# Expert rows in tiles of 256 and of 128 rows, and the second tile's weights loaded ahead of the wait for rows

## The reference

```
logits = x @ Wr.T                                  # 8 experts
scores = softmax(logits); the best two of 8 are kept
g = silu(x @ Wg[e].T); u = x @ Wu[e].T             # 512 -> 352 each
out_e = (g * u) @ Wd[e].T                          # 352 -> 512
routed = sum over the two kept experts of score * out_e
shared = (silu(x @ Wsg.T) * (x @ Wsu.T)) @ Wsd.T   # 704 hidden channels
x + gb * (routed + shared)
```

## Time and profile before

| | us |
|---|---|
| median of three runs | 1813.94 |
| the three runs | 1813.15, 1813.94, 1815.92 |
| span of the profiled execution | 1812.5 |
| PE busy | 1708.2 (94%) |
| DVE busy | 1336.2 (74%) |
| ACT busy | 768.1 (42%) |

### The profile page before, as it was taken

How to read it: one execution, slowest core, us unless ns; L and a number is a source line. 1 busy time by engine, 2 the same in 40 slices (tenths; PEclk the granted TensorE clock), 3 DMA queues, 4 the chain that set the end, 5 groups by cost and what they waited for, 6 DMA issues and landing times.

```text
span 1812.5 us, 28335 instructions
## 1 busy us (share of the span) xinstructions
PE 1708.2 (94%) x9093; PEld 1481.3 (82%) x9093; DVE 1336.2 (74%) x2564; ACT 768.1 (42%) x1151; POOL 413.5 (23%) x503
## 2 busy tenths in 40 slices
PE   5499999999779999999999998999999999999998
PEld 0388888888568888888887887999999999998888
DVE  4899999997588777787777654666666666666772
ACT  2333333333245454544454313555545555443331
POOL 0244444442122111322322340000000000004740
PEclk9699999999889999999999999999999999999999
DMA  8432222221624433645554696777767777665861
GB/s 333 132 130 87 78 90 93 87 75 64 212 99 151 154 126 122 215 170 185 182 193 172 226 350 239 269 247 269 258 244 263 247 269 258 243 242 170 293 214 38
DMA packets 141638, 339.31 MB, mean 187 GB/s; under 512 B 20664, under 2 KB 20664, under 8 KB 136048
## 3 DMA queue, kind: packets, MB, share of 16 engines
q1 hardware_dynamic: 110864, 250.68, 40.4%
q10 hardware_dynamic: 20448, 54.01, 7.9%
q0 software_dynamic: 10240, 33.56, 5.3%
HBM read 230.40 MB, written 107.79 MB: 187 GB/s over the span
## 4 chain that ended last, share of the span: by engine, by line
PE 78%; DVE 9%; DMA 6%; issue 3%; ACT 2%; SPq 1%; POOL 1%; ACTq 0%; DVEq 0%; POOLq 0%
PE bank L595 20%; PE bank L597 19%; PE bank L596 19%; PE bank L606 6%; PE bank L2106 4%; PE bank L2104 4%; PE bank L2105 3%; PE bank L2099 2%; DMA out<-raw 1%; DVE k_lo L1591 1%; DVE hid L1677 1%; DMA stage<-in_w_k 1%; ACT sg_t L1238 1%; DMA base<-xres_rows 1%; PE bank L2088 1%
## 5 line engine op out<-in xcount | busy, mean ns | idle before, releaser
L595 PE MATMUL bank<-gu_hi,ex_x_hl 128*128 128x352 f32 x1136 | 378.6, 333 | 1.9 <-DVE gu_lo L1873 1.8
L597 PE MATMUL bank<-gu_hi,ex_x_hl 128*128 128x352 f32 x1136 | 366.9, 323 | 0.0
L596 PE MATMUL bank<-gu_lo,ex_x_hl 128*128 128x352 f32 x1136 | 366.8, 323 | 0.0
L1677 DVE TENSOR_TENSOR hid<-bank,sg_t 128x352 f32<-128x352 f32 x142 | 74.4, 524 | 224.3 <-ACT sg_t L1238 224.3
L595 PEld LDWEIGHTS bank<-gu_hi,ex_x_hl 128*128 128x128 f32 x1136 | 214.4, 189 | 2.4 <-DVE gu_lo L1873 2.1
L596 PEld LDWEIGHTS bank<-gu_lo,ex_x_hl 128*128 128x128 f32 x1136 | 214.5, 189 | 0.0
L597 PEld LDWEIGHTS bank<-gu_hi,ex_x_hl 128*128 128x128 f32 x1136 | 214.0, 188 | 0.0
L1115 POOL DMA_INDIRECT raw<-expert_out_rows,out_slots x64 | 75.2, 1175 | 590.8 <-DMA expert_out_rows<-y_rows 567.8
L1238 ACT ACTIVATE sg_t<-bank 128x352 f32<-128x352 f32 x142 | 66.0, 465 | 273.1 <-PE bank L597 272.8
L2104 PE MATMUL bank<-dn_hi,hid_hi 128*128 128x512 f32 x426 | 170.4, 400 | 9.1 <-DVE hid_lo L1681 9.1
L2106 PE MATMUL bank<-dn_hi,hid_lo 128*128 128x512 f32 x426 | 168.7, 396 | 0.0
(11 more groups left out here) (230 smaller groups left out, 3879.6 us busy)
## 6 DMA issues: line engine op xcount, KB each, us to landing
raw<-in_ex_gu SPq DMA_DIRECT2D x39, 1408.0 KB, 6.9
raw<-in_ex_dn SPq DMA_DIRECT2D x39, 512.0 KB, 7.6
ex_x<-expert_in_rows SPq DMA_DIRECT2D x78, 256.0 KB, 2.8
expert_out_rows<-y_rows ACTq DMA_DIRECT2D x78, 256.0 KB, 4.0
h_rows<-h_t SPq DMA_DIRECT2D x64, 256.0 KB, 2.3
h_turned<-h_hl ACTq DMA_DIRECT2D x32, 512.0 KB
ex_x_hl<-h_turned ACTq DMA_DIRECT2D x32, 512.0 KB, 3.3
x_t<-in_x SPq DMA_DIRECT2D x32, 256.0 KB, 2.6
```

The lines of the kernel that those rows point to most:

```text
L595: pe.matmul(acc, act_hi[i], w_hi[i], start=(i == 0), stop=False)
L596: pe.matmul(acc, act_hi[i], w_lo[i], start=False, stop=False)
L597: last = pe.matmul(acc, act_lo[i], w_hi[i], start=False, stop=(i == chunks - 1))
L1677: dve.tensor_tensor(hid[:, half, 0:F], PS_U[bank][:, 0:F], sg_t[:], ALU.mult).then_inc(u_vec.sem_of["hid"], 1)
```

## The change

There are still 31 tiles of 256 rows (pairs), and 9 tiles of 128 rows (singles) join them: 71 units and 40 tiles instead of 78 and 39. Tiles 0 to 29 are pairs, 30 to 38 singles, 39 a pair. Each expert's rows are padded to a multiple of 128, its even part fills pairs as long as there are any, the rest goes to singles; the tables are computed for both kinds. The padding zeros are 128 rows per expert. Each tile's two parts of weights have semaphores of their own. Tile 1's weights are loaded in front of the wait for rows. The loop becomes a written-out list of units, in which `split_places` says in which unit each piece of weights is split, and on which side of `hid`. The buffers that the gathered outputs use are swapped (`cb_y1`, `cb_y2` to `raw[0]`, `cb_out` to `raw[1]`).

```diff
-NJ = (2 * N + E * (R - 1)) // R
-NU = NJ * R // P
+NU = (2 * N + E * (P - 1)) // P
+NPAIR = 2 * N // R - 1
+NSINGLE = NU - 2 * NPAIR
+NJ = NPAIR + NSINGLE
...
+def is_single(j):
+    return NPAIR - 1 <= j < NJ - 1
...
+LAST_OF = {j: units_of(j)[-1] for j in range(-2, NJ + 2)}
+FIRST_OF = {j: units_of(j)[0] for j in range(NJ + 2)}
+def split_places():
+    hi_first, hi_middle, lo_before, lo_after = ({u: [] for u in UNIT} for _ in range(4))
+    hi_first[ROUTED0 - 1].append((0, "gu"))
+    lo_before[ROUTED0 - 1].append((0, "gu"))
+    for j in range(NJ + 2):
+        u = FIRST_OF[j]
+        alone = is_single(j) or j >= NJ
+        if j and (is_single(j - 1) or j - 1 >= NJ):
+            hi_first[u].append((j, "dn"))
+            lo_after[u].append((j, "dn"))
+            if j + 1 < NJ + 2:
+                hi_middle[u].append((j + 1, "gu"))
+                lo_before[u + 1].append((j + 1, "gu"))
+        elif alone:
+            hi_first[u].append((j + 1, "gu"))
+            lo_before[u].append((j + 1, "gu"))
+        else:
+            hi_first[u].append((j + 1, "gu"))
+            lo_after[u].append((j + 1, "gu"))
+        if not alone:
+            hi_first[u + 1].append((j + 1, "dn"))
+            lo_after[u + 1].append((j + 1, "dn"))
+    return hi_first, hi_middle, lo_before, lo_after
...
@@ SP
             sp.wait_ge(route_done, 1)
-            load_expert(FIRST)
+            load_gu(0)
+            load_dn(0)
             sp.wait_ge(pads_zero, 1)
             for e in range(E):
                 pad_rows(e)
+            load_gu(1)
+            load_dn(1)
...
+            def routed_step(unit):
+                if unit.k + 3 < NU:
+                    load_rows(unit.k + 3)
+                if unit.begins and unit.load < FU:
+                    load_base(unit.load)
+                elif unit.begins and SPLIT <= unit.load < NT:
+                    load_residual(unit.load)
+                for j, part in LO_BEFORE[unit.u] + LO_AFTER[unit.u]:
+                    if j + 2 < NJ + 2:
+                        (load_gu if part == "gu" else load_dn)(j + 2)
...
@@ ACT
+            for u in range(ROUTED0, LATE0):
+                unit = UNIT[u]
+                for piece in HI_FIRST[u]:
+                    expert_hi(*piece)
+                if unit.k + 1 < NU:
+                    routed_x_hi(unit.k + 1)
+                hidhi(u - 1)
+                for piece in HI_MIDDLE[u]:
+                    expert_hi(*piece)
+                silu(u, unit.slot)
...
@@ DVE, tables
+            def running(values, out):
+                link(dve.tensor_tensor(summed[:], upto[:], values[:].to_broadcast([P, E, E]), ALU.mult))
+                link(dve.tensor_reduce(out[:, 0, :], summed[:], AX.X, ALU.add))
...
             def tile_tables():
-                cur = count["end" if E.bit_length() % 2 else "end2"]
+                padded, paired, single = (count[name] for name in ("padded", "paired", "single"))
+                pair_end, single_end = count["pair_end"], count["single_end"]
+                link(dve.tensor_tensor(single[:], padded[:], paired[:], ALU.subtract))
+                running(single, single_end)
+                link(dve.tensor_scalar(step_single[:], padded[:], -1.0, float(REGION), ALU.mult, ALU.add))
+                link(dve.tensor_tensor(step_single[:, :, 0:E - 1], step_single[:, :, 0:E - 1], paired[:, :, 1:E], ALU.add))
+                link(dve.tensor_scalar(step_single[:, :, E - 1:E], step_single[:, :, E - 1:E], float(SPARE_PAIRS * R), None,
+                                       ALU.add))
                 dve.wait_ge(table_const, 1)
-                link(dve.tensor_tensor(below[:], cur[:].to_broadcast([P, NJ, E]), first_row[:], ALU.is_le))
+                for ends, steps_of, p0, p1 in ((pair_end, step_pair, 0, NPAIR), (single_end, step_single, NPAIR, NJ)):
+                    here = [P, p1 - p0, E]
+                    link(dve.tensor_tensor(below[:, p0:p1, :], ends[:].to_broadcast(here), first_row[:, p0:p1, :], ALU.is_le))
+                    link(dve.tensor_tensor(steps_below[:, p0:p1, :], below[:, p0:p1, :], steps_of[:].to_broadcast(here),
+                                           ALU.mult))
                 link(dve.tensor_reduce(eid_f[:, :, 0], below[:], AX.X, ALU.add))
                 link(dve.tensor_scalar(eid_f[:], eid_f[:], float(E - 1), None, ALU.min))
                 link(dve.tensor_copy(eid[:], eid_f[:, :, 0]))
-                link(dve.tensor_tensor(steps_below[:], below[:], step[:].to_broadcast([P, NJ, E]), ALU.mult))
                 link(dve.tensor_reduce(row_f[:, :, 0], steps_below[:], AX.X, ALU.add))
                 link(dve.tensor_tensor(row_f[:, :, 0], row_f[:, :, 0], first_row[:, :, 0], ALU.add))
+                link(dve.tensor_tensor(row_f[:, NPAIR:NJ, :], row_f[:, NPAIR:NJ, :],
+                                       paired[:, :, 0:1].to_broadcast([P, NSINGLE, 1]), ALU.add))
+                begin_pair, begin_single = shift["pair"], shift["single"]
+                link(dve.tensor_tensor(begin_pair[:], pair_end[:], paired[:], ALU.subtract))
+                link(dve.tensor_tensor(begin_single[:], single_end[:], single[:], ALU.subtract))
+                link(dve.tensor_tensor(single_from[:], region[:], paired[:], ALU.add))
+                link(dve.tensor_scalar(begin_single[:], begin_single[:], float(NPAIR * R), None, ALU.add))
+                link(dve.tensor_tensor(begin_single[:], begin_single[:], pair_end[:], ALU.subtract))
+                link(dve.tensor_tensor(begin_pair[:, :, 1:E], single_end[:, :, 0:E - 1], padded[:, :, 0:E - 1], ALU.subtract))
+                link(dve.tensor_scalar(begin_pair[:, :, 1:E], begin_pair[:, :, 1:E], -1.0, -float(NPAIR * R + REGION),
+                                       ALU.mult, ALU.add))
+                link(dve.tensor_tensor(begin_pair[:, :, 1:E], begin_pair[:, :, 1:E], pair_end[:, :, 0:E - 1], ALU.add))
                 dve.tensor_copy(row_of_tile[:], row_f[:, :, 0]).then_inc(route_done, 1)
             def result_slots():
                 past = y_rows[:, 1, :].rearrange("p (n e) -> p n e", e=E)
+                every = [P, 2 * NT, E]
                 link(dve.tensor_copy(slot_f[:, :, 0], flat(slots[:])))
-                link(dve.tensor_scalar(next_region[:], region[:], float(REGION), None, ALU.add))
-                link(dve.tensor_tensor(past, slot_f[:].to_broadcast([P, 2 * NT, E]),
-                                       next_region[:].to_broadcast([P, 2 * NT, E]), ALU.is_ge))
-                link(dve.tensor_tensor(past, past, step[:].to_broadcast([P, 2 * NT, E]), ALU.mult))
-                link(dve.tensor_reduce(flat(route["sc"][:]), past, AX.X, ALU.add))
-                link(dve.tensor_tensor(slot_f[:, :, 0], slot_f[:, :, 0], flat(route["sc"][:]), ALU.subtract))
+                for froms, name, added in ((region, "pair", "sc"), (single_from, "single", "ex")):
+                    link(dve.tensor_tensor(past, slot_f[:].to_broadcast(every), froms[:].to_broadcast(every), ALU.is_ge))
+                    link(dve.tensor_tensor(past, past, shift[name][:].to_broadcast(every), ALU.mult))
+                    link(dve.tensor_reduce(flat(route[added][:]), past, AX.X, ALU.add))
+                for added in ("sc", "ex"):
+                    link(dve.tensor_tensor(slot_f[:, :, 0], slot_f[:, :, 0], flat(route[added][:]), ALU.add))
                 dve.tensor_copy(flat(out_slots[:]), slot_f[:, :, 0]).then_inc(slots_done, 1)
...
@@ DVE, routed units
+            for u in range(ROUTED0, LATE0):
+                unit = UNIT[u]
+                if unit.k + 1 < NU:
+                    x_lo(unit.k + 1)
+                hidlo_rows(u - 1)
+                for piece in LO_BEFORE[u]:
+                    expert_lo(*piece)
+                hid_of(u)
+                for piece in LO_AFTER[u]:
+                    expert_lo(*piece)
+                if unit.k:
+                    y_of_unit(unit.k - 1)
...
@@ PE, up() and the units
+                if unit.routed:
+                    pe.wait_ge(*x_vec.done(unit.k, "lo"))
+                    if unit.begins:
+                        pe.wait_ge(*rw_lo_vec.done(unit.load, "gu_lo"))
...
+            for u in range(EARLY0, UNITS):
+                if ROUTED0 <= u < LATE0 - 1:
+                    turn_rows(u + 1 - ROUTED0)
+                turn_hid(u - 1)
+                up(u)
...
+                down(u - 1)
```

More of the change, by code:

```diff
@@ L96, in only @@
         return self.pair is None and self.n == n
[L99 to L120, removed]
@@ L123, with singles_before, table_column @@
[L123 to L137, removed]
-UNITS = 2 * NT + NU
+def is_single(j):
+    return NPAIR - 1 <= j < NJ - 1
+def singles_before(j):
+    return sum(is_single(i) for i in range(j))
+def table_column(j):
+    return NPAIR + singles_before(j) if is_single(j) else j - singles_before(j)
@@ L1310, in expert_hi @@
-            def expert_hi(t, part):
-                last = (ROUTED.unit(t.back(2), 1) if t.pair is not None or t.n >= 2
```

(50 more changed lines are left out.)

556 lines of the change are left out of this document (282 added, 274 removed).

## The result

The changed kernel takes 1828.56 us (median of 4 runs, 1825.26 to 1832.04), the kernel before 1814.72 us beside it (4 runs, 1813.15 to 1815.92): a ratio of 1.0079 [1.0063, 1.0095], slower. Forecast were 1826.6 us and slower. The profiled execution has a span of 1827.2 us, where the one before had 1812.5, and a mean granted clock of 0.962 instead of 0.976.

The account below looks back on a forecast made before the run. PE was taken to bound the kernel. -46.6 + 45.8 + 16.8 + 0.1 - 3.4 = +12.7 us on the profiled 1812.5 us, plus 1.4 us around the span, gave 1826.6 us; range 1807 to 1843.

Parts of the forecast that it names:

- Fewer units: Routed part: 78 units become 71, each 6.65 us of PE's path, so 46.6 us less.
- Eight waits: Tiles 32 to 39: PE's `up` waits for `gu_lo`, 5.73 us added in each of 8 steps, 45.8 us.
- The clock: Behind each of the eight waits PE's clock falls, 2.1 us lost each time, 16.8 us in all.
- clock holds: Rival, block of singles: the clock stays up through the gaps; -6.2 us, 1807.7 us, faster; chance 0.11.
- lower clock throughout: Rival, block of singles: the clock doesn't come back between gaps; +46.5 us, 1860 us; chance 0.07.
- Where the routed part begins: Tables and first routed units: longer tables and their clock loss against the earlier load of tile 1; net +0.1 us.
- The tables: Ahead of the routed part: more DVE table work adds 5.7 us to PE's waits, plus 2.1 us of clock.
- It costs them some microseconds: Start of routed part: tile 1's load delays tile 0's rows, but PE needs them later, so nothing is lost.
- the -7.7 us of the load: First routed unit: tile 1's earlier load removes 5.1 us of PE's wait and 2.6 us of clock loss.
- The late part: Where the late part begins: the 1.84 us wait for `gu_lo` and its 1.6 us of clock go, -3.4 us.

Follow-up runs that it names:

- spread: Changed kernel with the same nine single tiles, each between pairs: 1766.65 us, 0.9737 of the kernel before; in a later session 1776.92 us, 0.9775.
- experiment 5: Kernel before with one call moved, tile 1's load ahead of the wait for rows: 1811.89 us, 0.9982 of the kernel before.
- experiment 2: Changed kernel with `gu_lo` of the next tile made one step earlier, behind `hid` of this unit: 1803.52 us, 0.9948 of the kernel before.
- experiment 7: Changed kernel with the table work in four pieces ahead of `hid` of early units 3 to 6: 1833.56 us, 1.0076 of the kernel before.
- both: Changed kernel with the edits of spread and experiment 7 together: 1773.32 us, 0.9732 of the kernel before.
- best: Kernel of both with the paddings issued once the counts are known, ahead of loads 0 and 1: 1765.73 us, 0.972 of the kernel before.
- experiment 6: Changed kernel with tile 1's load put back behind the rows of tile 0: 1833.44 us, 1.0066 of the kernel before.
- both_late: Kernel of both with tile 1's load behind the rows of tile 0: 1769.55 us, 0.9726 of the kernel before.
- experiment 9: The same kernel as best, both with the paddings issued ahead of loads 0 and 1: 1765.73 us, 0.972 of the kernel before.

## Why the prediction was right

**Fewer units, -46.6: right.** 280 matmuls are gone, and spread shows the whole sum arriving when nothing stands in its way.

**Eight waits, +45.8: right.** PE waits eight times 5.53 us, 44.2 in total; with the clock held up the steps are 46.2 us longer. The chain went link by link as the prediction has it. The one link off is its last, 3.19 us for 3.13. The list of waits says "issue" where I had announced `gu_lo`; the timeline shows `up` starting as `gu_lo` ends.

**The clock, +16.8: right, 1.6 too much.** It fell at eight of eight gaps and came back each time: 1.90 us in the mean where I had 2.1, the mean of 2.6 and 1.6. That the mean is so near is partly luck: single gaps cost from 1.3 to 2.8 us (steps of 13.7 to 15.3 less 12.43), wider than the two rows that it was taken from. The rule of the Trainium skill, TensorE: Matmul & The Clock Gate, section HAM oscillation — how this bites in real kernels, that a kernel that waits in every tile pays at each gap, holds here in all eight. At the 3.1 us gaps of experiment 2 it holds only in part: there some steps lost nothing. The rivals "clock holds" and "lower clock throughout" fall with the windows.

**Where the routed part begins, +0.1: the net is near (-1.0), its terms are not.** The tables were to cost 5.7 us of DVE's work and 2.1 us of clock, 7.8 in all; they cost 7.0. DVE's work grew by 5.8, as counted; 1.2 us are a longer wait for a transfer, which I didn't count; and the clock did fall, but its loss is not on the path, since DVE and not PE is late there. Two more steps failed. "It costs them some microseconds, and PE asks for these rows only after two or three more units, so nothing": with the load ahead PE waited 2.99 us for the rows in experiment 5. And the -7.7 us of the load were summed as if the tables' delay did not touch them: with load 1 late nothing is lost (6), with short tables nothing is gained (7). When the rows and tile 1's weights arrive is set by SP's list; what PE loses ahead of them is taken off its wait for them, so the two terms can't be added. That the errors cancel is luck.

**The late part, -3.4: half right.** The 1.84 us wait is gone; the clock fell at the 1.87 us wait for `hid` instead, and the `up` behind it takes 5.48 us (1676.28 to 1681.76) instead of 3.92: 1.6 us. I had counted a loss that goes with a gap as if it went for good.

**Around it.** The total is 2.0 us over the forecast, 1828.6 against 1826.6, and 3.0 us of the profiled pair lie in the start, before the change acts. That the agreement is that close is partly luck.

## What to carry to other kernels

When a tile is halved, its weights are due twice as often: look where their preparation stands in the engine's list, and put it a step ahead and into that engine's idle time in front of its next due piece, or keep two such tiles from following each other. Don't sum two gains that lie ahead of the same arrival; find the last arrival first, and ask what sets it. A lower clock cost nothing here where PE waited for DVE right behind it, at the tables. The clock's cost is told apart from the wait's by filling the gap with matmuls that nothing uses.

## What the hardware showed unexpectedly

- The same gap lowers the clock or not. At 5.5 us it fell eight times of eight. At 3.1 us (experiment 2) the first matmul behind the gap took 0.63 us three times and 0.40 us five times, and four of seven steps were 1.3 to 2.7 us longer, though the steps are alike in what PE does. At a gap of 1.8 to 1.9 us for `hid` in the late part it held before and fell after. At the tables it fell at a gap of 2.35 us in experiment 7 (0.50 in the next 2 us) and stayed at 1.00 at gaps of 2.34 and 2.35 us in 'both' and 'best'.
- Matmuls that nothing uses (20 of 512 columns in 4.82 us) kept it at 1.00 through a gap of the same length.
- A transfer of rows behind a weight load lands late. Tile 0's rows of 256 KB took 2.5 to 3.0 us from issue to landing with load 1 behind them (before, experiment 6, 'both_late'); with it in front they took 5.0 to 5.5 (the changed kernel) and 6.5 to 6.7 us (experiment 5), and 10.1 to 10.7 us with loads 0 and 1 in front (experiment 9).
- The first 1040 us, alike in all kernels of this case, end up to 4 us apart in the profiles, and two sessions of one kernel differ by 0.4% in their ratio to the kernel before; a difference under that between sessions says nothing.
